# Edge attributes of a graph attention layer: four neighbouring rows to a partition, turned by products with the identity

## What is computed

```
# layer 1
relevant = segment_sum(x[src] * w[:, None], dst)
x = layernorm(x + relevant @ W1 + (relevant * x) @ W2)
# layer 2: attention with 8 heads of 16
q, k, v = x @ Wq + bq, x @ Wk + bk, x @ Wv + bv
e = edge_attr @ We + be                  # edge_attr is [412500, 64]
logits = ((q[dst] * k[src]).sum(-1) + (q[dst] * e).sum(-1)) * SCALE
attn = softmax of logits over the edges of one dst
x = layernorm(x + segment_sum(attn * v[src], dst) @ Wo + bo)
```

## Time and profile before

| what | value |
|---|---|
| median of three runs | 13336.66 us |
| the profiled execution | 13459.18 us, its span 13456.0 us |
| mean granted TensorE clock | 0.715 of full speed |
| `attention`, groups 1 to 202 | about 6467 to 13230 us |
| busy in `attention`, of each 1000 us | PE 710, POOL 480, ACT 412, DVE 398, DMA engines 48% |

### The profile page before, as it was taken

How to read it: one execution, slowest core, us unless ns; L and a number is a source line. 1 busy time by engine, 2 the same in 40 slices (tenths; PEclk the granted TensorE clock), 3 DMA queues, 4 the chain that set the end, 5 groups by cost and what they waited for, 6 DMA issues and landing times. The chain is left out here.

```text
span 13456.0 us, 216744 instructions
## 1 busy us (share of the span) xinstructions
PE 7720.9 (57%) x45360; PEld 6286.5 (47%) x45360; DVE 4996.8 (37%) x19346; ACT 3854.0 (29%) x9042; POOL 8316.9 (62%) x6569
## 2 busy tenths in 40 slices
PE   2444444444444444445567777777777777777777
PEld 1333433334334343344455555555555555555555
DVE  2333333333333333335433433443343333334344
ACT  1111111111111111111244444444444444444444
POOL 3888888888888888884444444444444444444441
PEclk7666666666666666667777777777777777777776
DMA  8666666666666666666444444444444444444442
GB/s 195 106 106 106 105 107 106 105 107 106 106 106 106 106 106 106 106 106 179 142 135 134 135 133 136 135 134 133 135 134 134 135 134 135 134 137 134 132 135 81
DMA packets 2266464, 1665.00 MB, mean 124 GB/s; under 512 B 763524, under 2 KB 2024262, under 8 KB 2265830
## 3 DMA queue, kind: packets, MB, share of 16 engines
q0 software_dynamic: 628992, 668.10, 29.3%
q1 hardware_dynamic: 1631218, 963.68, 25.1%
q10 hardware_dynamic: 5877, 29.94, 0.6%
HBM read 1376.17 MB, written 284.55 MB: 123 GB/s over the span
## 5 line engine op out<-in xcount | busy, mean ns | idle before, releaser
L499 POOL DMA_INDIRECT rel_sum<-sums,row x3224 | 5003.7, 1552 | 1197.8 <-issue 641.4
L1125 POOL DMA_INDIRECT kv<-kv_rows,src_idx x3232 | 3234.9, 1001 | 3505.5 <-PE out_ps L1231 2482.8
L450 PE MATMUL coef_ps<-same,spread 128*128 128x128 f32 x6448 | 1629.6, 436 | 3542.5 <-DVE spread L418 2815.7
L450 PEld LDWEIGHTS coef_ps<-same,spread 128*128 128x128 f32 x6448 | 1421.3, 325 | 3717.1 <-DVE spread L418 2967.6
L432 DVE TENSOR_TENSOR row<-moved,src_col 128x8 int32<-128x8 f32 x403 | 69.2, 172 | 3784.3 <-DMA rel_sum<-sums,row 3784.3
L1160 PE MATMUL ring_ps<-pick,q_win 128*128 128x128 f32 x6464 | 1346.3, 371 | 127.2 <-issue 73.8
L1160 PEld LDWEIGHTS ring_ps<-pick,q_win 128*128 128x128 f32 x6464 | 1148.9, 267 | 481.1 <-issue 440.9
L478 ACT ACTIVATE sums<-sum_ps 128x512 f32<-128x512 f32 x806 | 437.7, 594 | 2893.8 <-DMA rel_sum<-sums,row 2892.3
L1225 PE MATMUL out_ps<-put,kv 128*128 128x128 f32 x6464 | 1154.7, 334 | 183.1 <-issue 103.6
L418 DVE TENSOR_SCALAR spread<-iota_n,rel_col,w_col 128x128 f32<-128x128 f32 x3224 | 1208.5, 379 | 0.0
L414 DVE SCALAR_TENSOR_TENSOR same<-src_bc,src_col,later 128x128 f32<-128x128 f32 x3224 | 1116.5, 346 | 177.9 <-issue 105.2
(11 more groups left out here) (172 smaller groups left out, 8213.4 us busy)
## 6 DMA issues: line engine op xcount, KB each, us to landing
q_win<-q_rows SPq DMA_DIRECT2D x3232, 64.0 KB
src_bc<-src_flat SPq DMA_DIRECT2D x403, 512.0 KB
x_win<-in_x SPq DMA_DIRECT2D x3224, 64.0 KB
rel<-rel_flat SPq DMA_DIRECT2D x202, 512.0 KB
attr<-in_edge_attr SPq DMA_DIRECT2D x804, 128.0 KB
kv<-kv_rows,src_idx POOLq DMA_INDIRECT x3232
mark<-marks SPq DMA_DIRECT2D x808, 64.0 KB
rel_sum<-sums,row POOLq DMA_INDIRECT x3224
```

Source lines behind the costliest of these rows:

```text
L450: last = nc.tensor.matmul(coef_ps[k][:, i, :], spread[:, b, j, :], same[:, b, j, :], start=True, stop=True)
L499: pool.indirect_dma_start(out=rel_sum[r], out_offset=bass.IndirectOffsetOnAxis(ap=row[:, b, j:j + 1], axis=0), in_=sums[:, b, j, :], in_of ...
L1125: pool.indirect_dma_start(out=kv[:, 2 * i + u, j, :], out_offset=None, in_=kv_rows, in_offset=bass.IndirectOffsetOnAxis(ap=src_idx[:, i, t ...
```

## The change

`attr` becomes [128, 2, 2, 4, 64], and the rows of a bank are handed out as `(q p s)`: partition p takes the four neighbouring edges 4p to 4p + 3 of the bank's 512, one run of 1 KB. So a DMA has 128 runs instead of 512; the number of DMAs (four a group) and their bytes stay. The last, partial group is loaded as whole partitions and a rest (`last_rows`).

A block `attr[:, u, h, s, :]` is now [128 partitions, 64 features] and holds edges 4p + s of bank h. `attr_fill` turns each by a plain product with the identity, out[64, 128] = block^T @ ident, for h = 0 to output partitions 0 to 63 and for h = 1 to 64 to 127: eight products of 64 columns in place of four transposes of 128. The result has its columns in the order (s, p); `attr_drain` writes `attr_t` in the order of the edges, (p, s), reading PSUM with a step of 128 floats. `keys` and all else stay.

```
     def load_attr
-  rows = edge_attr[bass.ds(n.g * AP, AP), :].rearrange("(q s p) f -> q p s f", q=B, p=P)
+  rows = edge_attr[bass.ds(n.g * AP, AP), :].rearrange("(q p s) f -> q p s f", q=B, s=S)
   for h in range(2):
-      sp.dma_start(attr[:, u, :, h, :], rows[2 * u + h]).then_inc(attr_in[u], 16)
+      sp.dma_start(attr[:, u, h, :, :], rows[2 * u + h]).then_inc(attr_in[u], 16)

     def attr_fill
   for s in range(S):
-      mm = nc.tensor.transpose(to[:, s, :], attr[:, u, s, :, :].rearrange("p h f -> p (h f)"), ident[:])
+      for h in range(2):
+          mm = nc.tensor.matmul(to[h * ED:(h + 1) * ED, s, :], attr[:, u, h, s, :], ident[:], start=True, stop=True)
   mm.then_inc(attr_filled[u], 1)

     def attr_drain
-  nc.scalar.activation(attr_t[:], ring_ps[place_of("attr", u)[0] % 2][:], ACT.Copy
+  turned = ring_ps[place_of("attr", u)[0] % 2][:].rearrange("f s p -> f p s")
+  nc.scalar.activation(attr_t[:].rearrange("f a b -> f (a b)").rearrange("f (p s) -> f p s", s=S),
+                       turned, ACT.Copy
                        ).then_inc(attr_drained[u], 1)
```

More of the change, by code:

```diff
@@ L891, in has, with last_rows @@
         return g.is_from(0) and g.is_under(NG)
+    def last_rows(u):
+        ends = [(h, LAST_ROW + (2 * u + h) * SP, max(0, min(SP, E - LAST_ROW - (2 * u + h) * SP))) for h in range(2)]
+        return [(h, at, n // S, n % S) for h, at, n in ends]
     with ExitStack() as ctx:
@@ L910, in attention @@
         kv = sb("kv", [P, 6, U, 2 * D])
-        attr = sb("attr", [P, 2, S, 2, ED])
+        attr = sb("attr", [P, 2, 2, S, ED])
         attr_t = sb("attr_t", [P, S, P])
@@ L1049, in load_attr @@
                     if n.is_under(NG - 1):
-                        rows = edge_attr[bass.ds(n.g * AP, AP), :].rearrange("(q s p) f -> q p s f", q=B, p=P)
+                        rows = edge_attr[bass.ds(n.g * AP, AP), :].rearrange("(q p s) f -> q p s f", q=B, s=S)
                         for h in range(2):
-                            sp.dma_start(attr[:, u, :, h, :], rows[2 * u + h]).then_inc(attr_in[u], 16)
+                            sp.dma_start(attr[:, u, h, :, :], rows[2 * u + h]).then_inc(attr_in[u], 16)
                     else:
[L1054 to L1062, removed]
+                        for h, at, full, more in last_rows(u):
+                            if full:
+                                sp.dma_start(attr[0:full, u, h, :, :], edge_attr[at:at + full * S, :].rearrange(
+                                    "(p s) f -> p s f", s=S)).then_inc(attr_in[u], 16)
+                            if more:
+                                rest = edge_attr[at + full * S:at + full * S + more, :]
+                                sp.dma_start(attr[full:full + 1, u, h, 0:more, :], rest.rearrange(
+                                    "(p s) f -> p s f", p=1)).then_inc(attr_in[u], 16)
                 def load_rel(n):
@@ L1143, in attr_fill @@
                     full = n.is_under(NG - 1)
-                    loads = 2 if full else sum(LAST_ROW + ((2 * u + h) * S + s) * P < E for s in range(S) for h in range(2))
+                    loads = 2 if full else sum((rows > 0) + (more > 0) for h, at, rows, more in last_rows(u))
                     if full:
```

## The result

The change took 14061.49 us (median of four runs, 14048.21 to 14071.03) against 13337.94 us before: a ratio of **1.0548** (95% interval 1.0526 to 1.0571), 724 us or 3.6 us a group. The forecast was 13459 us in a range up to 13700: the direction was right, the size six times too small. The profiled execution has a span of 14069.4 us, and what was added lies in the attention stage, which went from 6753 to 7363 us in the profiled executions (first to last fill). That is 3.0 us a group there, since the profiled execution of before was 0.9% above its median.

What follows compares the result with a forecast made beforehand. No engine is full; a loop of waits through POOL's gathers and PE's out_bank sets the period. +152 us on the path, -30 us for loads, +122 us on the median 13336.66 gave 13459 us, range 13240 to 13700.

Steps and rivals of the forecast that it cites:

- What of this is on the path: Step on how much added PE and ACT time in the attention stage lengthens the period: +0.75 us a group, +152 us.
- I count half: 0.25 us: Fill (m, 0), ahead of out_bank(c, 2) and out_bank(c, 3): half its added time delays POOL's second burst, 0.25 us.
- the sum had 13.6: Sign in the profile after: POOL's wait for out_bank up from 12.9 to about 13.6 us a group.
- The fill, +0.5 us: PE's two fills of a group: eight products, 16 records, take 1.16 us, +0.5 us a fill.
- The rival without overlap: The two halves of a PE fill run one after the other: +1.7 us a fill, 13700 us; chance 0.13.
- The drain, +0.49 us: ACT's two drains: reading with a step of 128 floats goes from 587 to 1080 ns, +0.49 us.
- The loads, -30 us: SP and DMA engines: longer runs save a third of PE's 95 us of waits for attributes, -30 us.
- The rival in which the loads decide: Shorter landing of attribute loads gains while added PE time is hidden: -100 us, 13237 us; chance 0.12.
- The fill of half 1 with its drain, +0.5 us a group, 101 us: Fill (m, 1) and its drain, ahead of keys(n, 1): half of 0.5 + 0.49 us counts, 0.5 us a group.
- Hidden altogether: Rival: PE's 3.2 us wait ahead of keys(n, 1) and late signals swallow the added time; 13307 us, chance 0.17.
- The clock: Rival: plain products keep PE's clock up in one group of two, giving back 202 us; 13257 us, chance 0.08.
- The bursts themselves: Sign: POOL's bursts stay as before; the forecast is wrong if they change or the period falls.

Runs made afterwards that it cites:

- e13: Kernel before plus 16 unread bf16 products between gather_ends(n) and spread_carry(n), slow chip: 14005.12 us against 13346.78, 1.0495.
- e16: The change with the fill of half 0 moved behind gather_ends(n) and 16 unread products behind that fill, slow chip: 14433.89 us, 1.082 of the kernel before.
- e18: Kernel before plus twelve tiny bf16 products of one moving column ahead of each fill's transposes, slow chip: 13716.69 us, 1.0295.
- e17: Kernel before plus one f32 product of 512 columns ahead of each fill's transposes, slow chip: 13406.1 us against 13324.52, 1.0059.
- e4: Kernel before plus twelve tiny bf16 products of one moving column ahead of each fill's transposes, quick chip: 11528.08 us, 1.0305.
- e5: The change itself, run on the quick chip: 11520.91 us against 11188.24 for the kernel before, 1.0299.
- e1: The change with four transposes instead of the products (attributes on wrong edges), quick chip: 11182.48 us against 11186.68 for the kernel before, 0.9996.
- e14: Kernel before with the eight products in the fill of half 1 alone, slow chip: 13434.52 us, 1.0072.
- e10: The change plus 16 unread bf16 products between gather_ends(n) and spread_carry(n), quick chip: 11151.83 us, 0.9968 of the kernel before.
- e15: The change plus 16 unread bf16 products between gather_ends(n) and spread_carry(n), slow chip: 14268.9 us, 1.0696 of the kernel before.
- e8: The change with the fill of half 0 moved from ahead of out_bank(c, 2) to behind gather_ends(n), quick chip: 11124.22 us, 0.9947 of the kernel before.
- e9: Kernel before with only the fill of half 0 moved behind gather_ends(n), quick chip: 11155.83 us against 11187.83, 0.9971.
- e6: Kernel before plus one f32 product of 512 columns ahead of each fill's transposes, quick chip: 11521.48 us, 1.0299.

## Why the prediction was wrong

**The step that failed** is the first half of "What of this is on the path": for the fill (m, 0) "I count half: 0.25 us" a group. I took a late signal as something that does not depend on what PE does in a burst, so only the 0.5 us of PE time could count. The runs on the slow chip show that products put ahead of a signal of PE in a burst make that signal late by far more than their own time (e13 and e16 for the signal of `spread_carry`, e18 and the change for that of `gather_ends`; e17 shows that the time alone does little). In the change the signal takes 6.4 us instead of 2.8, and the wait ahead of POOL's second burst goes from 3.5 to 7.5 us in the mean, where I had added 0.25 us. All of POOL's waits went from 12.9 to 16.0 us a group; the sum had 13.6. How much of it the products alone would cost on this chip was not run.

The trace of before had it: "Signals arrive late during a burst, and in bundles after it." I read the 2.3 us of one group as the second wait; in 24 of 179 groups of the same trace the signal of `gather_ends` took over 5 us and the wait was 8.7 us. The question I did not ask is which signal of the chain still got through, and by how much.

Point by point:

- *The fill, +0.5 us*: 16 records in 1.09 us against 0.65, +0.44 us of busy time, as forecast. But the next product comes 0.83 us later than before in half 1 and 0.40 us later in half 0; the 0.3 us of idleness behind 16 records was in no row. The halves of the columns work side by side, as the quarters did. The rival without overlap is refuted. With the Trainium skill's sentence on independent tiles ("TensorEngine Tiling (Array Packing)", Tiling Modes) the trace agrees: 16 records of half the columns in 1.09 us, eight full ones in 1.16. A drain when the mode changes can't be told apart here: e4, with no 64-column product, is followed by 0.43 us of the same idleness, e5 by 0.26 to 0.29.
- *The drain, +0.49 us*: median 579 ns against 580 before, nothing. The row I took as the nearest, L1721 with 1080 ns, writes with a step into SBUF; this one reads PSUM with one. I priced a read by a write. The Trainium skill's sentence on lines of PSUM ("SBUF — State Buffer", Door 1: The DMA port swizzle) speaks of matmuls; ScalarE's read shows no loss here.
- *The loads, -30 us*: q1 has 309,464 packets fewer (forecast 310,000), and PE's waits for attributes went from 95 to 36 us (18.3 + 17.8 in two waits), twice the gain I had put; whether it reached the time is not shown. e1 finds nothing gained on the quick chip; on the slow one the loads alone were not run. The rival in which the loads decide did not happen.
- *The fill of half 1 with its drain, +0.5 us a group, 101 us*: e14 measured 88 us for the fill alone. The size is right by luck: half of my term was the drain, which costs nothing, and the fill holds PE up for 0.83 us, not 0.5.
- *Hidden altogether*: refuted by the same run and by the result.
- *The clock*: that plain products would keep it up in the place of transposes is not borne out as a gain, though the clock is 0.01 to 0.02 higher. But the clock matters on the quick chip, by the gap behind `gather_ends`, a place I had not looked at.
- *The bursts themselves* did not change (0.95 us a gather, 0.30 between), nor did the period fall.

I also added the cost of one profiled execution of one chip. That the same kernel runs 16% faster on another chip, with another bound, could not be seen in the trace.

## What to carry to other kernels

When a trace shows signals that come late while POOL issues indirect DMAs, find the signal on which the loop turns, count over all groups how often it gets through, and look at what stands ahead of it on its engine: a few instructions more can move a whole chain behind the burst, at many times their own duration.

Price a block on PE by the distance from its start to the start of the next product, not by its busy time: 16 short records in 0.95 or 1.09 us took 1.38. A transposed f32 block is one record, a plain f32 product is two. And where PE is the bound, look at what it does just before its clock falls; work put into that gap can cost less than nothing, but only on the chip where this is the bound (e10: 0.3% faster than the kernel before on one, e15: 7% slower on the other).

No version here is better on both kinds of chip. e8 (0.9947 and 0.9956) is the fastest on the quick one; neither it nor e9 was run on the slow one.

## What I had not expected of the hardware

- Two chips run the attention stage at 33 and at 22 us a group with the same program, while the stages before it take the same time.
- On the slow chip a signal of PE is seen by DVE 7.2 us after the product that gives it, in a burst of POOL; on the quick one the same signal takes 0.8 us in the same kernel.
- Sixteen matmul records keep PE from its next product for 1.38 us, whether they are busy for 0.95 us (e4) or 1.09 us (e5). With e6's long product in the row, four kernels with different fills take the same time within 0.06% (11521 to 11528 us), at the same clock of 0.86.
- ScalarE reads PSUM with a step of 512 bytes at full pace (579 ns for 512 columns); its write with a step of 16 bytes took 1080 ns.
